# A two-layer hybrid network in one kernel: read products of two batches interleaved, old rows put earlier, last additions shared with GpSimd

## The chip, the cores and the metric

The kernel runs on one core of a Trainium2 chip. The core has five engines with instruction queues of their own: TensorE (PE; its weight loads are listed as PEld), VectorE (DVE), ScalarE (ACT), GpSimd (POOL) and SyncE (SP), which here only issues the stores. The metric is the device time of one launch in microseconds. Lower is better.

## What is computed

The input x has 4 batches of 512 rows of 256 numbers, all float32. Seven blocks follow one another, each of which adds its result to x: latent attention, a ternary feed-forward, cosine attention, the feed-forward again, gated linear attention, a *workspace block*, attention with low-rank adapters (the *adapter stage*), and the workspace block again. Only the workspace block is touched. Cut to what matters:

```
for _ in range(2):                                   # two rounds
    logits = rms(x, w_pre) @ compete_w.T + compete_b
    vals, idx = top_k(swapaxes(logits, 1, 2), 4)     # 4 rows chosen for each of 16 slots
    written = softmax(vals) * (x @ write_w.T + write_b)[idx]    (summed over the 4)
    ws = rms(ws + written, w_post)
    q, k, v = x @ wq.T, ws @ wk.T, ws @ wv.T         # 4 heads, keys and values are the 16 slots
    att = softmax(q k / sqrt(64))
    x = rms(x + (att v) @ out_w.T + out_b, w_post)
```

The block's input is the layer norm of the running x, and its output is added to the running x.

## The kernel before

`last_stages` (in the launch's last third) runs three programs one behind the other on every engine: the first workspace stage ("wsa"), the adapter stage, and the second workspace stage ("wsb"), which alone is given `out` and stores the result. Each engine has one queue, written out by hand; semaphores order the engines.

A workspace stage keeps the running x in `x` and the block's own rows in `xf` (the buffer appears in the profile as cos_wq), as 16 tiles of 128 rows by 256, 4 tiles to a batch. It runs WS_NB = 2 rounds. Round r works as follows on all four batches at once: turn the rows (`turn`, transposes L2289, copied by ScalarE in round 0 and by VectorE at L2045 in round 1), bid (`bid`, L2309), spread the row scales (L2299), select four rows for each slot, write the slots, fold the keys and values into small matrices, scores (L2385), turn the scores (L2393), take the maximum off (`shift`, VectorE), exponents (ScalarE), `divide` (VectorE), turn the probabilities (`turn_probs`, L2399, with the copy L2270 by ScalarE into `attT`), and read.

Reading adds the probabilities times the folded values to the old rows, in PSUM. A batch has two banks, `WS_TURN_BANKS[b]`, of two tiles each. `put_rows` (L2405) multiplies two tiles of old rows by the identity into one bank and so starts the sum. A bank is free at different times: the *early half* of each batch is put before the probabilities are turned, the *late half*, `WS_LATE_HALF[b]`, in `read`, because its bank holds turned scores (banks 2 and 3, for batches 0 and 2) or turned probabilities (banks 4 and 5, for batches 1 and 3) until then. The folded values and the probabilities of two batches, a pair, share the partitions of one buffer: the first batch has rows 0 to 63, the second rows 64 to 127. A float32 product is two instructions on TensorE, so a batch is read by 4 products, 8 instructions (L2413), of 64 rows each, and `put_rows` is 2 instructions.

Behind a batch's read, ScalarE squares and sums its four tiles from PSUM (`mean_squares`, L2228), GpSimd makes the row scales (`row_scales`, L2033 and L2035), and VectorE scales each tile (`norm_sum`, L2128). In round 0 the scaled tile goes to `xf` and the next round begins. In round 1 it stays in PSUM, and VectorE adds the four tiles to `x` with two additions (L2136); with `out` the batch is then stored by SyncE (L2008). The order of VectorE's queue is batch by batch: four scalings, two additions, then what the hooks put behind a batch. In the first stage these hooks are the adapter stage's row statistics (L61 and on) behind batches 0 and 2 and its normalised rows (L2673) behind batch 1.

The adapter stage opens on TensorE with 44 filler products (`keep_busy`, L2867), which first wait for batch 0's addition, then turns the rows (L2878) and makes q and k (L2888, four instructions for each tile, copied by ScalarE). GpSimd and VectorE rotate two tiles of q and k each (L2645, L2649, L2654).

At the very end GpSimd clears each semaphore of these stages (L54), 120 of them.

Of the kernel before, what the change touches and what calls it, by code (L numbers as in the profile page):

```python
# [9 lines left out]
ALU = mybir.AluOpType  # L10
# [4 lines left out]
P = 128  # L15
B, S, D = 4, 512, 256
TI = S // P
# [1877 lines left out]
WS_S, WS_K, WS_NB, WS_H = 16, 4, 2, 4  # L1895
# [12 lines left out]
WS_LATE_HALF = (1, 0, 1, 0)  # L1908
# [25 lines left out]
def workspace_programs(k, g, slots, ps, tag, early, out=None, free=None, hooks={}):  # L1934


    x, ident = g["x"], g["ident"]
    own, shared = slots.own, slots.shared

    def hook(name, *args):  # L1940
        if name in hooks:
            hooks[name](*args)
# [4 lines left out]
    xf = g["cos_wq"][:, :, :].rearrange("p c d -> p (c d)").rearrange("p (n d) -> p n d", d=D)  # L1947
# [25 lines left out]
    nb_w = shared("nb", [P, 2, D])  # L1973
# [6 lines left out]
    attT = shared("attT", [P, 2, S])  # L1980
# [3 lines left out]
             "written", "wsum_ready", "wss_ready", "wsr_ready", "ws_ready", "wt_ready", "wsT_ready", "kv_ready",  # L1984
             "kbd_ready", "vbd_ready", "m_ready", "m_copied", "cb_ready", "cb_copied", "nb_ready", "nb_copied",
             "a_ready", "a_copied", "at_ready", "ash_ready", "ae_ready", "att_ready", "pt_ready", "attT_ready",
             "xb_ready", "m2_ready", "r2_ready", "x_ready", "stored")
    s = {n: k.sem(f"{tag}_{n}") for n in names}
    bias = g["ws_in_b"]

    def tiles(b):
        return slice(b * TI, (b + 1) * TI)

    def bank(n):
        return ps[:, n, :]
# [4 lines left out]
    def read_tile(b, i):  # L2000
        return bank(read_bank(b, i // 2))[:, (i % 2) * D:(i % 2 + 1) * D]

    def by_sync(sp):
        if out is None:
            return
        for b in range(B):
            sp.wait_ge(s["x_ready"], b + 1)
            sp.dma_start(out[b, :, :].rearrange("(i p) d -> p i d", p=P), x[:, tiles(b), :])\  # L2008
              .then_inc(s["stored"], 16)
        sp.wait_ge(s["stored"], 16 * B)  # L2010
# [21 lines left out]
    def row_scales(pool, kind, b):  # L2032
        pool.tensor_tensor(mse[:, kind, tiles(b)], msq[:, kind, tiles(b)], g["ws_eps"][:, 0:TI], ALU.add)  # L2033
        pool.drain()  # L2034
        return pool.tensor_tensor(inv[:, kind, tiles(b)], mse[:, kind, tiles(b)], g["neg_half"][:, 0:TI], ALU.pow)  # L2035

    def first_scales(pool, b):
        pool.wait_ge(s["msq_ready"], b + 1)
        row_scales(pool, 0, b).then_inc(s["inv_ready"], 1)

    def by_vector(dve):
        def copy_turned(r, b):
# [80 lines left out]
        def norm_sum(r, b):  # L2123
            dve.wait_ge(s["r2_ready"], r * B + b + 1)
            for i in range(TI):
                n = b * TI + i
                rows_out = xf[:, n, :] if r + 1 < WS_NB else read_tile(b, i)
                last = dve.scalar_tensor_tensor(rows_out, read_tile(b, i), inv[:, 1, n:n + 1],  # L2128
                                                g["ws_post"][:, :], ALU.mult, ALU.mult)
            if r + 1 < WS_NB:  # L2130
                last.then_inc(s["xf_ready"], 1)
                return
            dve.drain()
            for h in range(2):
                at = b * TI + 2 * h
                last = dve.tensor_tensor(x[:, at:at + 2, :],  # L2136
                                         bank(read_bank(b, h)).rearrange("p (i d) -> p i d", i=2),
                                         x[:, at:at + 2, :], ALU.add)
            last.then_inc(s["x_ready"], 1)
# [41 lines left out]
    def by_gpsimd(pool):  # L2181
        nh, eps = g["neg_half"], g["ws_eps"]

        def slot_scales(r):
            pool.wait_ge(s["wss_ready"], r + 1)
            pool.tensor_tensor(wse[:, :], wss[:, :], eps[:, 0:1], ALU.add)
            pool.drain()
            pool.tensor_tensor(wsr[:, :], wse[:, :], nh[:, 0:1], ALU.pow).then_inc(s["wsr_ready"], 1)

        if early == 0:  # L2190
            pool.memset(vbd[:, :, :, :, :], 0.0)
            invert_variance(pool, 0)
            invert_variance(pool, 1)
            for b in range(B):
                if b + 2 < B:
                    invert_variance(pool, b + 2)
                first_scales(pool, b)
        else:
            for b in range(early, B):
                invert_variance(pool, b)  # L2200
                first_scales(pool, b)
        hook("gpsimd_opened", pool)
        for r in range(WS_NB):
            if r > 0:
                for b in range(B):
                    pool.wait_ge(s["msq_ready"], r * B + b + 1)
                    row_scales(pool, 0, b).then_inc(s["inv_ready"], 1)
            slot_scales(r)
            if r + 1 < WS_NB:
                pool.wait_ge(s["ws_ready"], r + 1)  # L2210
                pool.tensor_tensor(wsb[:, :], ws[:, :], g["ws_write_b"][:, :], ALU.add).then_inc(s["wsb_ready"], 1)
            for b in range(B):
                pool.wait_ge(s["m2_ready"], r * B + b + 1)
                row_scales(pool, 1, b).then_inc(s["r2_ready"], 1)
                if r + 1 == WS_NB:
                    hook("gpsimd_after_batch", pool, b)
            pool.drain()

    def by_scalar(act):
# [55 lines left out]
    def by_tensor(pe):  # L2275
# [120 lines left out]
        def turn_probs(r, q):  # L2396
            pe.wait_ge(s["att_ready"], 2 * r + q + 1)
            for i in range(TI):
                last = pe.transpose(bank(4 + q)[:, i * P:(i + 1) * P], att[:, q, i, :], ident[:, :])  # L2399
            last.then_inc(s["pt_ready"], 1)  # L2400

        def put_rows(r, b, half):

            at = b * TI + 2 * half
            pe.matmul(bank(read_bank(b, half)), ident[:, :], xf[:, at:at + 2, :].rearrange("p i d -> p (i d)"),  # L2405
                      start=True, stop=False)

        def read(r, b):
            q, b2 = b // 2, b % 2
            pe.wait_ge(s["attT_ready"], 2 * r + q + 1)  # L2410
            put_rows(r, b, WS_LATE_HALF[b])
            for i in range(TI):
                last = pe.matmul(read_tile(b, i), attT[64 * b2:64 * b2 + 64, q, i * P:(i + 1) * P],  # L2413
                                 nb_w[64 * b2:64 * b2 + 64, q, :], start=False, stop=(i % 2 == 1))
            last.then_inc(s["xb_ready"], 1)

        if early == 0:
            keep_busy(48, 7)
        for r in range(WS_NB):
            for b in range(B):  # L2420
                turn(r, b)
            bid(r)
            spread_scales(r)
            select(r)
            write(r)
            fold_outputs(r)
            scores(r, 0)
            scores(r, 1)
            turn_scores(r, 0)
            turn_scores(r, 1)  # L2430
            pe.wait_ge(s["nb_copied"], r + 1)
            for b in range(B):
                put_rows(r, b, 1 - WS_LATE_HALF[b])
            turn_probs(r, 0)
            turn_probs(r, 1)
            for b in range(B):
                read(r, b)

    return {"s": s, "by_sync": by_sync, "by_vector": by_vector, "by_gpsimd": by_gpsimd, "by_scalar": by_scalar,
            "by_tensor": by_tensor, "statistics": statistics, "scale_rows": scale_rows,  # L2440
# [835 lines left out]
```

## Time and profile before

| | before |
|---|---|
| median of 3 runs | 2189.97 us (2189.81 to 2190.53) |
| the profiled execution's own time | 2190.11 us |
| its span in the profile | 2188.4 us, 30020 instructions |
| mean granted TensorE clock | 0.969 |
| busy: PE, DVE, ACT, POOL | 1965.3, 1023.3, 812.9, 515.5 us |

The time of an execution is 1.7 us more than its span. "Busy" is the union of an engine's instructions over the span. Times in the rows are microseconds from the span's start, those of single instructions in a group's mean are nanoseconds. A row of the timeline has the start, the duration from the first instruction of a merged run to the end of its last, the engine, the line, the operation, out<-in with shapes, the number of instructions, and in brackets how long the engine was idle before and for whom. The clock column is 1.00 at 2.4 GHz and 0.50 at 1.2 GHz.

### The profile page before, as it was taken

How to read it: one execution, taken by the hardware profiler on the slowest of the kernel's cores; microseconds unless marked ns; L12 is line 12 of the kernel's file. 1: busy time of each engine (PE TensorE's matmuls, PEld its weight loads, DVE VectorE, ACT ScalarE, POOL GpSimd, SP SyncE). 2: the span in 40 equal slices, each digit the busy share in tenths (PEclk: the TensorE clock that was granted, in tenths of full speed). 3: DMA queues.
4: the chain of work that ended last, by engine and by line, in shares of the span. 5: the costliest groups of instructions: out<-in, count | busy, mean ns of one | idle time of the engine just before them, and what ended most of it. 6: DMA issues, size and time to landing. Idle time of an engine off the chain costs nothing. (4 is left out here: it accounts for less than half of the span.)

```text
span 2188.4 us, 30020 instructions
## 1 busy us (share of the span) xinstructions
PE 1965.3 (90%) x11522; PEld 1251.4 (57%) x11522; DVE 1023.3 (47%) x2231; ACT 812.9 (37%) x1786; POOL 515.5 (24%) x617
## 2 busy tenths in 40 slices
PE   6999999999899999999999999669857899999885
PEld 4556666566566766676677667523235554545653
DVE  4555555545223233333243322259955565556444
ACT  2554535545234233323332333135413234445332
POOL 2332322323001011111111010026631143542221
PEclk9999999999999999999999999879979999999998
DMA  5000000000200000000000000020000000000001
GB/s 224 1 1 1 1 1 1 1 1 1 74 1 1 1 1 1 1 1 1 1 1 1 1 1 1 1 69 0 0 1 1 1 1 1 1 1 2 1 1 39
DMA packets 9773, 24.01 MB, mean 11 GB/s; under 512 B 2449, under 2 KB 6305, under 8 KB 8865
## 3 DMA queue, kind: packets, MB, share of 16 engines
q1 hardware_dynamic: 8336, 18.92, 2.4%
q10 hardware_dynamic: 1296, 3.18, 0.4%
q8 instruction: 93, 1.52, 0.3%
q14 instruction: 48, 0.39, 0.1%
HBM read 20.00 MB, written 2.10 MB: 10 GB/s over the span
## 5 line engine op out<-in xcount | busy, mean ns | idle before, releaser
L1429 PEld LDWEIGHTS cos_ps<-cos_vx,cos_probs 128*128 128x128 f32 x2048 | 238.8, 191 | 33.6 <-issue 28.7
L1429 PE MATMUL cos_ps<-cos_vx,cos_probs 128*128 128x129 f32 x2048 | 239.8, 275 | 4.2 <-DVE cos_on L1158 4.2
L1420 PE MATMUL cos_ps<-lead_room,cos_kT 128*128 128x512 f32 x512 | 232.0, 598 | 7.4 <-PEq L50 6.1
L1322 ACT ACTIVATE cos_probs<-cos_ps 128x512 f32<-128x512 f32 x256 | 150.9, 598 | 186.7 <-PE cos_ps L1420 185.9
L671 ACT ACTIVATE probs<-sc,nmax 128x512 f32<-128x512 f32 (+3 forms) x256 | 132.3, 524 | 168.8 <-DVE nmax L525 166.7
L1244 POOL TENSOR_TENSOR cos_qrs<-cos_qse,neg_half 128x4 f32<-128x4 f32 x59 | 59.4, 1006 | 511.9 <-DVE cos_qse L1140 511.9
L780 PE MATMUL sc<-kT,qT 128*128 128x512 f32 (+3 forms) x512 | 172.2, 458 | 3.9 <-DVE probsT L537 2.6
L1420 PEld LDWEIGHTS cos_ps<-lead_room,cos_kT 128*128 128x128 f32 x512 | 94.8, 192 | 104.2 <-issue 101.5
L2743 DVE TENSOR_REDUCE cos_wq<-tail_ps 128x2 f32<-128x1024 f32 (+3 forms) x128 | 101.8, 823 | 82.4 <-PE tail_ps L2983 81.3
L1138 DVE TENSOR_REDUCE cos_qss<-cos_qsq 128x4 f32<-128x512 f32 x59 | 40.5, 686 | 194.4 <-ACT cos_qsq L1301 194.4
L752 PE MATMUL pq<-xnT,wap 128*128 128x512 f32 x256 | 124.9, 611 | 3.5 <-DVE swp L517 3.5
L525 DVE TENSOR_REDUCE nmax<-sc 128x1 f32<-128x512 f32 (+3 forms) x256 | 111.9, 483 | 28.8 <-PE sc L782 26.3
L2971 PE MATMUL tail_ps<-lora_kT,lora_qT 32*128 32x256 f32 (+3 forms) x512 | 105.8, 490 | 13.9 <-DVE cos_wq L2743 4.3
L1451 PE MATMUL cos_ps<-cos_wout,cos_onT 128*128 128x256 f32 x512 | 115.7, 379 | 0.0
L780 PEld LDWEIGHTS sc<-kT,qT 128*128 128x128 f32 x512 | 80.9, 192 | 60.1 <-issue 58.8
L1293 ACT ACTIVATE lead_room<-cos_ps 128x512 f32<-128x512 f32 x59 | 35.2, 597 | 211.9 <-PE cos_ps L1399 211.9
L1408 PE MATMUL cos_ps<-cos_wq,lead_room 128*128 128x512 f32 x236 | 111.0, 592 | 0.0
L2847 ACT ACTIVATE room<-tail_ps 128x768 f32<-128x768 f32 (+1 forms) x96 | 84.6, 881 | 68.8 <-PE tail_ps L2976 68.5
L605 POOL TENSOR_TENSOR rot<-swp,ropeT 128x512 f32<-128x512 f32 x32 | 40.6, 1267 | 272.2 <-DVE swp L517 272.2
L2976 PE MATMUL tail_ps<-lora_qT,lora_kT 32*128 32x256 f32 (+3 forms) x512 | 104.2, 484 | 0.0
L1451 PEld LDWEIGHTS cos_ps<-cos_wout,cos_onT 128*128 128x128 f32 x512 | 95.2, 190 | 13.2 <-issue 1.6
L1697 POOL TENSOR_TENSOR gla_qs<-gla_st,gla_qT 128x512 f32<-128x512 f32 x64 | 82.6, 1313 | 74.3 <-DVE gla_st L1637 74.3
(431 smaller groups left out, 3444.6 us busy)
## 6 DMA issues: line engine op xcount, KB each, us to landing
onT<-in_mla_wqT SPq DMA_DIRECT2D x1, 2048.0 KB, 9.8
lead_room<-in_mla_wo SPq DMA_DIRECT2D x1, 2048.0 KB, 20.1
cos_wq<-in_cos_wq SPq DMA_DIRECT2D x1, 2048.0 KB, 25.7
cos_wout<-in_cos_wout SPq DMA_DIRECT2D x1, 2048.0 KB, 7.4
out<-x SPq DMA_DIRECT2D x4, 512.0 KB, 2.9
x<-in_x SPq DMA_DIRECT2D x1, 1536.0 KB, 15.3
wq_pe<-in_mla_wq_pe ACTq DMA_DIRECT2D x1, 1024.0 KB, 14.8
x<-in_x SPq DMA_DIRECT2D x1, 512.0 KB, 4.2
```

What stands on the lines that cost most here:

```text
L525: red = dve.tensor_reduce(nmax[:, j, qi:qi + 1], sc[:, j, at:at + (qi + 1) * P], AX.X, ALU.max, negate=True)
L671: ex = act.activation(probs[:, j, at:at + (qi + 1) * P], sc[:, j, at:at + (qi + 1) * P], ACT.Exp, bias=nmax[:, j, qi:qi + 1], accum_out=ls ...
L752: last = pe.matmul(pq[:, :], wap[:, c, p, kind, :], xnT[:, b % 2, c, :], start=(c == 0), stop=(c == DC - 1))
L780: pe.matmul(sc[:, j, at:at + (qi + 1) * P], qT[:, n % 2, j, qi * P:(qi + 1) * P], kT[:, b % 2, j, 0:(qi + 1) * P], start=True, stop=False)
L1322: act.activation(probs[:, n % 2, kj, :], ps[:, kj, :], ACT.Exp).then_inc(s["e_done"], 1)
L1408: last = pe.matmul(ps[:, banks["project", b, u], :], xnT[:, b % 2, c, i * P:(i + 1) * P], wq[:, c, 512 * hq:512 * (hq + 1)], start=(c == 0 ...
L1420: pe.matmul(ps[:, kj, :], kT[:, b % 2, kj * P:(kj + 1) * P], qT[:, hq % 2, h % 4, :], start=True, stop=True).then_inc(s["s_ready"], 1)
L1429: last = pe.matmul(po[:, qi // 2, qi % 2, :], probs[:, n % 2, kj, qi * P:(qi + 1) * P], vx[:, b % 2, kj, :], start=(kj == 0), stop=(kj == ...
L1451: last = pe.matmul(y[i], onT[:, n % 2, a, :], wout[:, 8 * half + a, :], start=(half == 0 and a == 0), stop=(half == 1 and a == 7))
L2743: last = dve.tensor_reduce(qs[:, batch % 2, qi, h:h + 2, LORA_HD], ps[:, at:at + 2, col:col + n], AX.X, ALU.max, negate=True)
L2971: pe.matmul(ps[:, at + j, col:col + w], qT[r:r + LORA_SLOT, qi * P:(qi + 1) * P], kT[r:r + LORA_SLOT, n % 2, 0:w], start=True, stop=False)
L2976: turned = pe.matmul(ps[:, at + 2 + j, col:col + w], kT[r:r + LORA_SLOT, t % 2, kj * P:(kj + 1) * P], qT2[r:r + LORA_SLOT, kj * P:], start ...
```

## The change

Three things, in both workspace stages unless said otherwise.

1. `read` is replaced by `read_pair`: for each of the four tiles the product of the pair's first batch and that of its second alternate, instead of all four of one batch and then all four of the next. Each batch still signals `xb_ready` on its last product.
2. The late half of batches 0 and 2 is put before `turn_probs` of its pair, behind a wait for `ash_ready` (the shifted scores have been taken out of that bank). The late half of batches 1 and 3 stays right ahead of the pair's read.
3. In the last round of the second stage alone, the scaled tiles 2 and 3 of a batch are written to `xf` and not to PSUM; VectorE does one addition (tiles 0 and 1) and GpSimd the other (`add_half`, tiles 2 and 3). GpSimd's additions stand one batch late in its queue: behind the row scales of batch b comes the addition of batch b - 1, and that of batch 3 at the end. SyncE waits for both before it stores a batch. Each stage has two more semaphores.

```
-             "xb_ready", "m2_ready", "r2_ready", "x_ready", "stored")
+             "xb_ready", "m2_ready", "r2_ready", "x_ready", "stored", "sums_scaled", "x_added")
...
             sp.wait_ge(s["x_ready"], b + 1)
+            sp.wait_ge(s["x_added"], b + 1)
...
+    def add_half(pool, b):
+        if out is None:
+            return
+        pool.wait_ge(s["sums_scaled"], b + 1)
+        at = slice(b * TI + 2, b * TI + 4)
+        pool.tensor_tensor(x[:, at, :], xf[:, at, :], x[:, at, :], ALU.add).then_inc(s["x_added"], 1)
...
-                rows_out = xf[:, n, :] if r + 1 < WS_NB else read_tile(b, i)
+                to_rows = r + 1 < WS_NB or (out is not None and i >= 2)
+                rows_out = xf[:, n, :] if to_rows else read_tile(b, i)
...
+            if out is not None:
+                last.then_inc(s["sums_scaled"], 1)
             dve.drain()
-            for h in range(2):
+            for h in range(2 if out is None else 1):
...
                     hook("gpsimd_after_batch", pool, b)
+                    if b > 0:
+                        add_half(pool, b - 1)
+            if r + 1 == WS_NB:
+                add_half(pool, B - 1)
...
-        def read(r, b):
-            q, b2 = b // 2, b % 2
+        def read_pair(r, q):
             pe.wait_ge(s["attT_ready"], 2 * r + q + 1)
-            put_rows(r, b, WS_LATE_HALF[b])
+            put_rows(r, 2 * q + 1, WS_LATE_HALF[2 * q + 1])
             for i in range(TI):
-                last = pe.matmul(read_tile(b, i), attT[64 * b2:64 * b2 + 64, q, i * P:(i + 1) * P],
-                                 nb_w[64 * b2:64 * b2 + 64, q, :], start=False, stop=(i % 2 == 1))
-            last.then_inc(s["xb_ready"], 1)
+                for b2 in range(2):
+                    last = pe.matmul(read_tile(2 * q + b2, i), attT[64 * b2:64 * b2 + 64, q, i * P:(i + 1) * P],
+                                     nb_w[64 * b2:64 * b2 + 64, q, :], start=False, stop=(i % 2 == 1))
+                    if i == TI - 1:
+                        last.then_inc(s["xb_ready"], 1)
...
-            turn_probs(r, 0)
-            turn_probs(r, 1)
-            for b in range(B):
-                read(r, b)
+            for q in range(2):
+                pe.wait_ge(s["ash_ready"], 2 * r + q + 1)
+                put_rows(r, 2 * q, WS_LATE_HALF[2 * q])
+                turn_probs(r, q)
+            for q in range(2):
+                read_pair(r, q)
```

## Rows read from the trace of the kernel before

**Rows 1.** Waits, 2100 to 2121 us: who waited for whom, us in total, times, longest.
```profile
ACT room L2228 <- PE tail_ps L2413: 5.9, 4, 2.2
```

**Rows 2.** Timeline, first workspace stage, round 0: puts, reads, first squares.
```profile
1675.55 1.99 PE L2413 MATMUL tail_ps<-room 64*128 64x256 f32 x8
...
1677.47 1.13 PE L2405 MATMUL tail_ps<-cos_wq,ident 128*128 128x512 f32 x2
1677.58 0.38 ACT L2228 ACTIVATE room<-tail_ps 128x256 f32<-128x256 f32 x1 [2.19 <-PE tail_ps L2413]
...
1678.53 1.99 PE L2413 MATMUL tail_ps<-room 64*128 64x256 f32 x8
```

**Rows 3.** Timeline, the same round's end: last batch's squares, copies, bid.
```profile
1686.51 0.38 ACT L2228 ACTIVATE room<-tail_ps 128x256 f32<-128x256 f32 x1 [1.23 <-PE tail_ps L2413]
...
1688.34 0.42 ACT L2228 ACTIVATE room<-cos_wq 128x256 f32<-128x256 f32 x1
...
1691.47 4.88 DVE L2045 COPY cos_wout<-tail_ps 128x512 f32<-128x512 f32 x8
...
1696.49 3.64 PE L2309 MATMUL tail_ps<-cos_wout,wsp_cw 128*32 128x512 f32 x16 [3.97 <-DVE cos_wout L2045]
```

**Rows 4.** Timeline, 1701 to 1703 us: the adapter folds and the fillers behind.
```profile
1701.41 1.14 PE L2696 MATMUL tail_ps<-lora_b,lora_am 64*128 64x256 f32 x8
...
1702.48 0.34 PE L2279 MATMUL tail_ps<-mask_b,ident_b 128*128 128x128 bf16 x3
```

**Rows 5.** Timeline, second stage, round 1: early puts, turned probabilities, late put.
```profile
2151.10 3.60 PE L2405 MATMUL tail_ps<-cos_wq,ident 128*128 128x512 f32 x8
...
2155.10 0.66 PE L2399 MATMUL tail_ps<-ident,room 128*128 128x128 f32 x4 [0.40 <-DVE room L2119]
...
2157.38 1.02 PE L2405 MATMUL tail_ps<-cos_wq,ident 128*128 128x512 f32 x2
```

**Rows 6.** Timeline, second stage, round 1: batch 0's chain, and the last additions.
```profile
2160.36 0.38 ACT L2228 ACTIVATE room<-tail_ps 128x256 f32<-128x256 f32 x1 [2.19 <-PE tail_ps L2413]
...
2162.18 0.20 POOL L2033 TENSOR_TENSOR wsp_mse<-wsp_msq,ws_eps 128x4 f32<-128x4 f32 x1 [23.18 <-ACT room L2228]
...
2163.58 1.67 DVE L2128 SCALAR_TENSOR_TENSOR tail_ps<-tail_ps,wsp_inv,ws_post 128x256 f32<-128x256 f32 x4 [6.75 <-POOL wsp_inv L2035]
...
2165.32 1.29 DVE L2136 TENSOR_TENSOR x<-tail_ps,x 128x512 f32<-128x512 f32 x2
...
2174.69 1.29 DVE L2136 TENSOR_TENSOR x<-tail_ps,x 128x512 f32<-128x512 f32 x2
```

**Rows 7.** Timeline, first stage's last round and the adapter stage's opening.
```profile
1741.76 1.41 DVE L61 BATCH_NORM_STATS2 lora_stats<-x 128x6 f32<-128x256 f32 x4
...
1744.26 2.63 PE L2867 MATMUL tail_ps<-mask_b,ident_b 128*128 128x128 bf16 x44
...
1748.34 1.09 PE L2878 MATMUL tail_ps<-ident,lead_room 128*128 128x128 f32 x8 [1.45 <-DVE lead_room L2673]
...
1750.26 7.11 PE L2888 MATMUL tail_ps<-lead_room,lora_xnT 128*128 128x512 f32 x16 [0.83 <-ACT lora_xnT L2824]
...
1754.49 1.30 POOL L2645 TENSOR_TENSOR lora_rot<-lead_room,lora_rope 128x512 f32<-128x512 f32 x1
...
1755.07 1.29 DVE L2136 TENSOR_TENSOR x<-tail_ps,x 128x512 f32<-128x512 f32 x2
...
1756.49 1.21 DVE L2645 TENSOR_TENSOR room<-lead_room,lora_rope 128x512 f32<-128x512 f32 x1
...
1757.29 1.00 POOL L2654 TENSOR_TENSOR cos_wq<-lora_rot 128x256 f32<-128x256 f32 x1
```

**Rows 8.** Busy time by window: length, PE, PEld, DVE, ACT, POOL, then clock, DMA, GB/s.
```profile
1694.10:1697.60 3.50, 1.11 (x8) 0.46 (x12) 2.24 (x4) 1.86 (x9) 2.41 (x4) 0.51 0.02 5
```

**Rows 9.** Page, part 6, the stores: KB each, us from issue to landing.
```profile
out<-x SPq DMA_DIRECT2D x4, 512.0 KB, 2.9
```

**Rows 10.** Clears of semaphores, 2170 to 2189 us: ns min/median/max, first and last start.
```profile
L54 POOLq EVENT_SEMAPHORE_RANGE_CLEAR  x120: 44/44/44, 2179.3 to 2188.0; - x120
```

## The prediction

> **What bounds the kernel now.** The edits touch the two workspace stages alone, some 1620 to 1756 us and 2050 to 2188 us, of two rounds each. So I read, in this order, who waits for whom at the end of a round, the timeline there, and the granted clock. The waits at the end of the second stage's round 0 show ScalarE waiting for TensorE's read products once for each of the four batches, 5.9 us in all [rows 1]. The timeline says why: per batch TensorE puts the late half of the old rows (L2405, 1678.53 - 1677.47 = 1.06 us) and then reads (L2413, 1677.47 - 1675.55 = 1.92 us); the sum of 2.98 us is also the distance of ScalarE's batches, (1686.51 - 1677.58) / 3 = 2.98 us [rows 2, 3]. Where ScalarE does not wait, its four squares of a batch take 1688.34 - 1686.51 = 1.83 us. So in round 0 of either stage TensorE sets the end, and all that follows hangs on the last batch: VectorE scales batch 3, copies the turned rows for 4.88 us, and TensorE, idle for 3.97 us, bids [rows 3]. In the last round of all VectorE sets the end: scalings and both additions come every (2174.69 - 2165.32) / 3 = 3.12 us, which is more than TensorE's 2.98 [rows 6].
>
> **The read by pairs.** The 8 products of a batch use 64 of the array's 128 rows and stream one behind the other: 1.92 us, which I read as eight times 0.213 us (half of the 0.427 us that a 512-column product takes, below) and 0.21 us before the next kind. After the change 16 products alternate between upper and lower 64 rows. The trace has this shape in this order: the adapter folds (L2696), 64x256, alternating halves, into two banks. Eight of them take 1702.48 - 1701.41 = 1.07 us to the next instruction, four times 0.213 and the same 0.21 [rows 2, 4]. So a pair costs 8 x 0.213 + 0.21 = 1.92 us, as much as one batch does now. The bounds are 1.92 (full overlap) and 16 x 0.213 + 0.21 = 3.62 us (none); I take 1.92, since the folds are the nearest row.
>
> In the first stage's times: batches 0 and 1 are read from 1675.55 to 1677.47, so batch 0 is ready when it is now; 2 and 3 are done at 1677.47 + 1.06 + 1.92 = 1680.45. ScalarE wants batch 2 at 1677.58 + 2 x 1.83 = 1681.24, so it waits no more, and its batch 3 starts at 1683.07 instead of 1686.51, 3.44 us sooner. GpSimd (2163.58 - 2162.18 = 1.40 us a batch) and VectorE (1.67) keep up with 1.83; the copies behind them move whole [rows 2, 3, 6]. The rows are turned for the next round with more room between, which may lower the clock; at half of it a batch takes 1.7 us to turn, and VectorE comes to batch 3 only after six of its eight copies (3.7 us). Two such rounds: **6.88 us**.
>
> **Rows that enter sooner.** The late halves of batches 0 and 2 move ahead of the turned probabilities. The early instructions start at 2151.10 in steps of 3.60 us for eight less the last one's tail, 0.427 each, so the tenth ends at 2151.10 + 10 x 0.427 = 2155.37, and the first transposes, now at 2155.10, come 0.3 us late. ScalarE's copy of them then ends near 2156.7 and is needed only behind the put that stays (2157.38). The new wait, on the shifted scores, never holds: VectorE shifts both pairs before it divides the first, whose transposes these are. Cost 0; without the cover it is 0.3 us a round. A gain has no place, as the read starts behind the second pair's transposes now and then [rows 5].
>
> **The last round of the first stage.** VectorE is the bound here, with additions and the adapter stage's statistics in one queue until 1755.07 + 1.29 = 1756.36. It starts with batch 0, which is not sooner: gain 0, though the last reads end 6 us earlier. A price can come from the clock. The 44 fillers, now at 1744.25 for 2.63 us right behind the reads, start as soon as batch 0's addition is done (1741.7, the statistics follow it) and end at 1744.3; the transposes still come at 1748.34. TensorE then idles for 4.0 us instead of 1.45 [rows 7]. Behind the idle time of 3.97 us ahead of the bid the granted clock stood at 0.51, the 1.2 GHz level [rows 3, 8]. If it falls here too, the transposes end about 0.9 us late, and a product pair of q and k (four instructions, 1.71 us) takes 3.4 us. The first two feed GpSimd's rotation (1754.49) and VectorE's (1756.49); their copies are ready some 0.9 us behind the products, near 1750.26 + 1.71 + 0.9 = 1752.9 and 1754.6, so 1.6 and 1.9 us ahead. Bounds: 0 (covered) and 5 us (all 16 products at half clock); I take **-0.3 us**, near the cover.
>
> **The last round of all.** VectorE's batch becomes 1.67 + 0.07 + 0.69 + 0.09 = 2.52 us, with one addition of 0.69 in place of two. GpSimd adds the other half from SBUF, 128x512: 1.30 us by L2645 of that shape; from above 2 x 1.00 = 2.00 us (L2654, half as wide), from below VectorE's 0.69 [rows 6, 7]. Behind the new wait in GpSimd's queue stand the row scales of the batches after, for which VectorE waits. With ScalarE's batches from 2160.36 every 1.83: GpSimd has scales 0 and 1 by 2163.58 and 2165.41, adds 0 until 2166.7, scales 2 (2168.1), adds 1 (2169.4), scales 3 (2170.8), adds 2 (2172.1). VectorE starts batch 3 at 2163.58 + 3 x 2.52 = 2171.14, its scalings end at 2172.81, and GpSimd's last addition at 2174.15. Now the last one ends at 2174.69 + 1.29 = 2175.98: **1.83 us** sooner. At 2.00 us an addition GpSimd becomes the bound and ends at 2176.3, 0.3 us later than now.
>
> Does GpSimd slow VectorE? Two additions from PSUM took VectorE 1.29 us while GpSimd multiplied from 1754.49 on, as long as in the last round; a product of two SBUF operands beside GpSimd took 1.21 us [rows 6, 7]. The Trainium skill's GPSIMD Engine Reference (Key points) has GpSimd share its SBUF interfaces with VectorE and contend with VectorE instructions that have two SBUF inputs. By that rule the changed loop is clear, since its scalings and additions take their other operand from PSUM; did they count as such, the second half of the batch would grow and the 1.83 us shrink toward nothing. The trace agrees with the rule.
>
> The stores come at least 1.9 us apart instead of 3.1, and one takes 2.9 us to land; if none may overlap, the last is some 0.9 us late. I take 0, since much of 2.9 us for half a megabyte must be the way there [rows 9]. Four more semaphores are cleared at the end, where 120 take 2188.0 - 2179.3 = 8.7 us: 4 x 0.073 = **-0.29 us** [rows 10].
>
> **Sum.** 6.88 + 1.83 - 0.3 - 0.29 = 8.1 us off the profiled execution: its span from 2188.4 to 2180.3, its time from 2190.11 to 2182.0. The median of the runs shown is 0.14 us under that time; I forecast 2181.9.
>
> **Rivals.**
> - *Each change of half drains the array*, with the 0.21 us seen at a change of kind [rows 2, 4]. Eight changes in a pair: 3.41 + 8 x 0.21 = 5.1 us. ScalarE's batch 3 in round 0 then starts at 1675.55 + 2 x 5.1 + 1.06 + 0.11 + 1.83 = 1688.75, 2.2 us later (twice); the first stage's last round starts 3.2 later, the last one ends 1.8 later, clears 0.3: 2190.1 + 9.7 = 2199.8, slower. It decides from a pair of 3.7 us up, where the gains at the round ends are used up by the late first batch. Against it: eight folds in 1.07 us leave no room for a drain. The skill's page TensorEngine Tiling (Key Properties) lets a change of tiling mode drain the engine, but not a change of tile; by it the pair stays at 1.92. Chance 0.04.
> - *No overlap, no drain*: 3.62 us a pair. Round 0 gains 0.7 twice, the first stage's last round loses 1.7, the last gains 1.2, clears 0.3: 2189.5, no change. The same row speaks against it. 0.05.
> - *The clock takes part back*: the adapter stage opens at 1.2 GHz for longer than the cover lasts. For it: 4.0 us of idle time, as ahead of the bid [rows 3, 8]. Against it: 1.6 to 1.9 us of cover. 2 to 5 us: 2184 to 2187. 0.15.
> - *The clock gives*: bid and spread of scales run from 1696.49 to 1701.41 at 1.2 GHz now [rows 3, 4, 8]; other gaps ahead of them might keep 2.4 GHz, worth some 2 us a round: 2178 to 2180. Against it: the idle time right before the bid stays. 0.06.
> - *The last additions give nothing*, by a slower GpSimd or stores in line: 2183 to 2184. 0.10.
> - *As forecast*, 2180.5 to 2183.3: 0.60.
>
> **Numbers.** A difference under 0.2% (4.4 us) counts as none: the line is at 2185.6. Faster are the forecast, the last additions, the clock that gives, and 0.12 of the clock that takes: 0.88. Same: its other 0.03 and no overlap, 0.08. Slower: 0.04. The range of 2179.5 to 2185.5 leaves out the two overlap rivals and the ends of the two of the clock, 0.16 together.
>
> **What would show it.** The 16 reads of a pair in about 2 us and two batches ready together; ScalarE's squares every 1.83 us, with no wait after the first; the copies of the turned rows 3.4 us sooner behind batch 0's read; in the last round VectorE every 2.5 us, GpSimd's additions near 1.3 us and the last of them ending the work; 124 clears. It would be wrong by a first batch that is ready later than now, by VectorE slowed while GpSimd adds, by TensorE, GpSimd or VectorE waiting longer at the adapter stage's opening, or by stretches of 0.50 where the clock now is 1.00.

## The result, and the profile after

The changed kernel took 2186.62 us (median of 12 executions, 2181.72 to 2190.11), the kernel before beside it on the same chip 2191.17 us (12, 2188.73 to 2195.46). The medians differ by 4.55 us (0.21%), the means by 5.3 us. The ratio of the means is 0.9976, 95% interval 0.9966 to 0.9985: faster by 0.24%, and the prediction's line for a change, 0.2%, lies inside that interval. The forecast was 2181.9 us, 2179.5 to 2185.5: the direction is right, the time 4.7 us too low and 1.1 us outside the range. The profiled execution took 2188.3 us, its span is 2186.4 us.

First the steps one by one. Waits of the changed kernel from 2100 to 2121 us, the answer to [rows 1]:

```profile
ACT room L2244 <- PE tail_ps L2430: 2.2, 1, 2.2
```

ScalarE waits for read products once, no longer four times. The timeline of the changed kernel, first workspace stage, round 0, answers to [rows 2, 3]:

```profile
1672.30 4.46 PE L2421 MATMUL tail_ps<-cos_wq,ident 128*128 128x512 f32 x10
...
1679.54 2.00 PE L2430 MATMUL tail_ps<-room 64*128 64x256 f32 x16
...
1681.46 1.12 PE L2421 MATMUL tail_ps<-cos_wq,ident 128*128 128x512 f32 x2
1681.56 0.39 ACT L2244 ACTIVATE room<-tail_ps 128x256 f32<-128x256 f32 x1 [2.18 <-PE tail_ps L2430]
...
1682.52 2.00 PE L2430 MATMUL tail_ps<-room 64*128 64x256 f32 x16
...
1687.06 0.39 ACT L2244 ACTIVATE room<-tail_ps 128x256 f32<-128x256 f32 x1
...
1692.02 4.88 DVE L2054 COPY cos_wout<-tail_ps 128x512 f32<-128x512 f32 x8
...
1697.04 3.59 PE L2325 MATMUL tail_ps<-cos_wout,wsp_cw 128*32 128x512 f32 x16 [3.97 <-DVE cos_wout L2054]
```

Sixteen products of a pair take 1681.46 - 1679.54 = 1.92 us to the next instruction, just the sum's figure, and ScalarE's squares come every (1687.06 - 1681.56) / 3 = 1.83 us, batch by batch. From batch 0's squares to the copies it is 1692.02 - 1681.56 = 10.46 us; before it was 1691.47 - 1677.58 = 13.89 [rows 2, 3]. The round gives 3.43 us of the 3.44. But the copies themselves start 0.55 us *later* than in [rows 3]: this execution came into the stage late. The last round of all answers to [rows 5, 6]:

```profile
2150.54 4.46 PE L2421 MATMUL tail_ps<-cos_wq,ident 128*128 128x512 f32 x10
...
2159.80 0.39 ACT L2244 ACTIVATE room<-tail_ps 128x256 f32<-128x256 f32 x1 [2.18 <-PE tail_ps L2430]
...
2163.03 0.88 DVE L2138 SCALAR_TENSOR_TENSOR tail_ps<-tail_ps,wsp_inv,ws_post 128x256 f32<-128x256 f32 x2 [6.75 <-POOL wsp_inv L2036]
...
2163.82 0.87 DVE L2138 SCALAR_TENSOR_TENSOR cos_wq<-tail_ps,wsp_inv,ws_post 128x256 f32<-128x256 f32 x2
...
2164.78 0.69 DVE L2148 TENSOR_TENSOR x<-tail_ps,x 128x512 f32<-128x512 f32 x1
2164.78 1.26 POOL L2048 TENSOR_TENSOR x<-cos_wq,x 128x512 f32<-128x512 f32 x1
...
2165.56 0.88 DVE L2138 SCALAR_TENSOR_TENSOR tail_ps<-tail_ps,wsp_inv,ws_post 128x256 f32<-128x256 f32 x2
...
2172.36 1.26 POOL L2048 TENSOR_TENSOR x<-cos_wq,x 128x512 f32<-128x512 f32 x1 [1.23 <-DVE cos_wq L2138]
```

VectorE's batch is 2165.56 - 2163.03 = 2.53 us (2.52 in the sum), GpSimd's addition 1.26 (1.30). Two scalings take 0.88 us where that addition runs beside them for 0.48 us (2165.56) and 0.88 without it (2163.03), so no slowing of VectorE shows. The last addition ends 2172.36 + 1.26 - 2159.80 = 13.82 us behind the first squares, before 2174.69 + 1.29 - 2160.36 = 15.62 [rows 6]: 1.80 us sooner, the sum says 1.83. The clears of the changed kernel and, from its page, its stores:

```profile
L54 POOLq EVENT_SEMAPHORE_RANGE_CLEAR  x124: 44/44/44, 2177.0 to 2186.0; - x124
```
```profile
out<-x SPq DMA_DIRECT2D x4, 512.0 KB, 3.0
```

Clearing takes 9.0 us instead of 8.7 [rows 10], and a store 3.0 instead of 2.9 [rows 9]. So each of these terms has its size. The term that has not is the clock's, at the adapter stage's opening, here in the timeline of the changed kernel, beside [rows 7],

```profile
1742.76 2.63 PE L2887 MATMUL tail_ps<-mask_b,ident_b 128*128 128x128 bf16 x44 [3.36 <-DVE x L2148]
...
1749.37 1.97 PE L2898 MATMUL tail_ps<-ident,lead_room 128*128 128x128 f32 x8 [3.98 <-DVE lead_room L2693]
...
1752.12 8.56 PE L2908 MATMUL tail_ps<-lead_room,lora_xnT 128*128 128x512 f32 x16 [0.78 <-ACT lora_xnT L2844]
...
1756.24 1.29 POOL L2665 TENSOR_TENSOR lora_rot<-lead_room,lora_rope 128x512 f32<-128x512 f32 x1 [0.69 <-ACT lead_room L2846]
```

and its windows there (busy time per engine, then the clock):

```profile
1742.80:1745.40 2.60, 2.59 (x44) 2.42 (x44) 2.45 (x11) 0.84 (x4) 0.42 (x1) 1.00 0.00 0
...
1749.30:1751.40 2.10, 1.97 (x8) 1.57 (x8) 2.03 (x6) 0.62 (x2) 2.02 (x2) 0.50 0.00 0
```

The fillers end early, TensorE idles 3.98 us (4.0 foreseen), and the turns run at a granted clock of 0.50, which is 1.2 GHz: 1.97 us instead of 1.09, q and k 8.56 instead of 7.11. GpSimd's rotation now waits 0.69 us for its copy. The larger part is that code which the change does not touch ran later. Windows of the kernel before, and below it of the changed kernel, over the block ahead of the first workspace stage:

```profile
1600.00:1620.00 20.00, 9.84 (x24) 5.21 (x20) 4.18 (x6) 4.97 (x6) 2.48 (x2) 0.69 0.00 0
1400.00:1620.00 220.00, 162.43 (x512) 59.97 (x512) 158.51 (x236) 78.99 (x123) 98.21 (x78) 0.88 0.05 18
```
```profile
1600.00:1620.00 20.00, 9.21 (x16) 4.23 (x17) 6.17 (x11) 4.97 (x6) 4.97 (x4) 0.54 0.00 0
1400.00:1620.00 220.00, 164.16 (x504) 59.61 (x505) 156.96 (x233) 79.13 (x123) 98.20 (x78) 0.85 0.06 18
```

Clock 0.85 instead of 0.88, eight products fewer done by 1620 us, and the first row statistics of the workspace stage start at 1620.46 us before and here at

```profile
1625.58 1.41 DVE L61 BATCH_NORM_STATS2 wsp_stats<-x 128x6 f32<-128x256 f32 x4 [1.99 <-PEq L50]
```

5.12 us late in unchanged code. The stages themselves, from these statistics to the end of the span, take 2186.4 - 1625.6 = 560.8 us against 2188.4 - 1620.5 = 567.9: 7.1 us less. The experiments ask whether the 5 us and the lost 1 us belong to the change.

### The profile page after: what moved, and what is told of

It is laid out like the page before. It is cut to its first block and busy times, and to the rows that moved or that the text cites. A ratio compares the mean times of both kernels' runs of the same rounds, so it can differ in the third digit from the quotient of the medians.

```text
span 2186.4 us, 30028 instructions
## 1 busy us (share of the span) xinstructions
PE 1958.1 (90%) x11522; PEld 1247.1 (57%) x11522; DVE 1021.8 (47%) x2227; ACT 815.1 (37%) x1786; POOL 521.1 (24%) x621
```

## Experiments

Two kinds of kernel were run. Full ones compute everything. *Cut* ones leave out the first five blocks: x and the weights are loaded and the three last stages start at once (first row statistics at some 22 to 23 us), so they show the stages without what lies ahead. "Mean" is over all executions of a run; a profiled execution is one of them. Times of runs are medians, with the lowest and highest in brackets.

**The stages alone, before and after.** The cut kernel before, and the cut changed kernel:

> The kernel before without its first 1620 us: latent, cosine and gated attention and both feed-forwards are left out, x and the weights are loaded, and the two workspace stages and the adapter stage run on the input x itself. It is the yardstick for the other cut kernels: some 575 us (2188.4 - 1620.5 us of stages and 10 to 20 us of loads). Spread theory (the 8.1 us are there, and what the whole kernel's medians miss comes from the stretch ahead of the first workspace stage, 5.1 us longer in the profile after): the executions of this kernel lie within 2 us of each other, where those of the whole kernel spread over 7. Clock theory (part of the gain goes back to the granted clock inside these stages): they spread by more than 3 us.

> The changed kernel with the same first stages left out. Spread theory: 8 us (7.5 to 8.6) less than the cut kernel before. Clock theory: 4.5 to 6 us less, with the missing part in stretches at 1.2 GHz at the opening of the adapter stage (TensorE's wait between the fillers and the transposes 4.0 us instead of 1.5).

593.41 us (589.88 to 595.31, 5 executions) and 583.51 (581.50 to 586.42, 4). The spread theory's 2 us is wrong: the executions of one kernel lie 5.4 and 4.9 us apart inside these stages too. The medians differ by 9.9 us, the means by 9.1, more than either theory says. The profiled spans are 588.2 and 579.8: 8.4 us less, where the sum has 8.1. The granted clock of the two is not the same. From their pages, 40 equal slices each, the kernel before first (a digit is the granted clock in tenths; 8 or less is a slice with a stretch at 1.2 GHz):

```profile
PEclk9979997999987998999999999999999999979995
```
```profile
PEclk9979987998798998999999999999999998889975
```

But every stretch outside the changed rounds takes the same time within 0.2 us, so the 8.4 us are the changed rounds'. Both were run once more, on further chips:

> The cut kernel before once more: five executions had a mean of 592.9 us, and eight of the cut changed kernel 584.4 us. Chance theory: the joint mean of this one stays within 592 to 594 us, 8 to 9 us over the cut changed kernel. Systematic theory (the changed stages lose more to the clock than the stages before): 590 to 591 us, 6 us over it.

> The cut changed kernel once more. Its four executions so far had a mean of 583.7 us, 9.2 us under the five of the cut kernel before. Chance theory: the joint mean stays 7.5 to 9.5 us under it. Systematic theory: it goes to 5 to 7 us.

590.25 (588.07 to 593.25) and 585.08 (583.77 to 586.39). Taken together 9 executions before have a mean of 591.8 and 8 after of 584.4: 7.4 us less, with a 95% interval of some 2.2 us either way. That lies between the two theories and decides nothing. The profiled spans of this second pair, 586.4 and 582.0, are only 4.4 us apart. Most of the missing 4 us are one stretch of unchanged code behind the first stage's last round, which took the kernel before 48.97 us here and 52.89 in its first profile (the changed kernel 53.06 and 52.93).

**The whole kernels again.** The changed kernel twice and the kernel before once more, on three further chips:

> The changed kernel as it is, once more, to set its mean against more executions of the kernel before on the same chip. Chance theory (the stages give 8.4 us, and the 12 executions on record were unlucky in the unchanged stretch ahead): the mean of these lies 7 to 9 us under that of the kernel before. Systematic theory (something outside the stages takes 3 us back): 4 to 6 us under it.

> The changed kernel once more, for six more executions beside the kernel before. Two profiled executions at the same position of the clock's changes differ by 8.0 us, two at different positions by 2.0 us. Chance theory: with these the difference of the means comes to 6.5 to 8 us. Systematic theory (other positions cost the changed kernel more than the kernel before): it stays at 5 to 6.5 us.

> The kernel before, unchanged, for a second profiled execution of it. Three profiled executions of the changed kernel reach the first workspace stage, in code that is the same in both kernels, at 1620.8, 1624.7 and 1625.6 us; the one of the kernel before at 1620.5. Chance theory: this one lies anywhere from 1620 to 1626, and the mean of its executions at 2191.9 within 2 us. Systematic theory (the change makes the stretch ahead longer): 1620.5 again, within 0.5 us.

The changed one took 2184.30 (ratio 0.9961, 0.9947 to 0.9975) and 2184.10 (0.9962, 0.9949 to 0.9975), in the mean 8.4 and 8.1 us under the kernel before on the same chip; the kernel before against itself has 0.9993 (0.9984 to 1.0002). The windows of the changed kernel's first repeat show the clock of the kernel before in the unchanged block, not that of the execution above:

```profile
1600.00:1620.00 20.00, 10.18 (x24) 5.24 (x20) 4.40 (x8) 4.97 (x6) 2.48 (x2) 0.69 0.00 0
1400.00:1620.00 220.00, 162.53 (x512) 60.01 (x512) 158.75 (x237) 78.97 (x123) 98.18 (x78) 0.88 0.06 18
```

Its statistics start at 1620.80 and its span is 2180.3, 8.1 us less than the 2188.4 of before; the stages take 559.5 us instead of 567.9, 8.4 us less as in the first pair of cut kernels. In the other repeats the statistics start at 1624.71 (changed) and 1622.18 (before), and the stages take 559.7 and 567.9 us. The changed kernel alone thus enters the stages anywhere from 1620.8 to 1625.6 us, so its late entry on record is scatter; the two profiles of the kernel before are 1.7 us apart. Over all runs 71 executions of the kernel before have a mean of 2192.1 (standard deviation 2.3), 24 of the changed one 2185.3 (2.8): 6.8 us less, within 1.3. All three expectations come out as the chance theories say.

**The parts alone**, in three cut kernels: the pairs and the sooner rows, with all last additions on VectorE (the third part of the change is taken out); the sooner rows alone; and all but the pairs. First the edit of the rows alone, in the kernel before:

```
-            put_rows(r, b, WS_LATE_HALF[b])
+            if b2 == 1:
+                put_rows(r, b, WS_LATE_HALF[b])
...
+                pe.wait_ge(s["ash_ready"], 2 * r + q + 1)
+                put_rows(r, 2 * q, WS_LATE_HALF[2 * q])
                 turn_probs(r, q)
```

And the single reads, which stand in place of `read_pair`'s products in the changed kernel:

```
+            for b2 in range(2):
+                if b2 == 1:
+                    put_rows(r, 2 * q + 1, WS_LATE_HALF[2 * q + 1])
+                for i in range(TI):
+                    last = pe.matmul(read_tile(2 * q + b2, i), attT[64 * b2:64 * b2 + 64, q, i * P:(i + 1) * P],
+                                     nb_w[64 * b2:64 * b2 + 64, q, :], start=False, stop=(i % 2 == 1))
+                last.then_inc(s["xb_ready"], 1)
```

> Cut kernel with the pairs and the earlier rows, but VectorE does all the last additions as before. My sum: the last round gains nothing (VectorE's 3.12 us a batch from the same start) and no semaphores are added, so 6.9 us less than the cut kernel before and 1.5 us more than the cut changed kernel. Rival: GpSimd's additions were hidden anyway, and it is as quick as the cut changed kernel.

> Cut kernel before with the rows of batches 0 and 2 put sooner and nothing else: batches are read singly. My prediction gave this part no gain of its own. If it has none, this is as slow as the cut kernel before. Rival, seen in the single reads above: batch 0 is ready one put (1.06 us) sooner and batch 3 two puts (2.1 us), so 2.1 us in each round 0 and 1.0 us in each last round where VectorE sets the end: 6.3 us less than the cut kernel before.

> The cut changed kernel without the pairs: rows sooner and the last additions shared, but every batch read singly, batch 0 and 2 ahead of the put that remains. With the rows alone a round 0 took 2.86 us less than before and with the pairs as well 3.46 us. Theory that the pairs pay little: 0.6 us more in each round 0, 0.87 us less in the first stage's last round and 0.4 us less in the last, so within 0.5 us of the cut changed kernel (stages of 559.5 us at the same clock). Rival, my prediction's (all of the 6.9 us come from the pairs): 6 us more than it.

They took 584.31 us (579.62 to 586.83), 585.03 (581.16 to 586.86) and 581.38 (578.91 to 588.88; 580.83 without that slowest one). Single executions of one kernel lie up to 10 us apart, so times can't tell the parts apart. Distances between rows of the timeline can, since they repeat within 0.05 us from profile to profile. All figures are in us, from one profile each, and the last column is a full kernel, further down:

| | before | rows | rows, pairs | rows, additions | changed | best |
|---|---|---|---|---|---|---|
| round 0 (each), early puts to copies | 23.16 | 20.30 | 19.70 | 20.29 | 19.70 | 19.70 |
| first stage's last round, early puts to first squares | 9.27 | 8.41 | 9.27 | 8.41 | 9.27 | 8.41 |
| last round, early puts to last store | 24.91 | 24.06 | 24.91 | 22.81 | 23.16 | 22.75 |
| first row twice, and the others | 80.50 | 73.07 | 73.58 | 71.80 | 71.83 | 70.56 |

The timeline of the rows alone says how they give 2.86 us without any pair (first stage, round 0; the cut kernel's times):

```profile
77.47 1.99 PE L2414 MATMUL tail_ps<-room 64*128 64x256 f32 x8
...
79.39 1.12 PE L2405 MATMUL tail_ps<-cos_wq,ident 128*128 128x512 f32 x2
...
80.45 2.96 PE L2414 MATMUL tail_ps<-room 64*128 64x256 f32 x16
...
83.34 1.12 PE L2405 MATMUL tail_ps<-cos_wq,ident 128*128 128x512 f32 x2
...
84.40 1.99 PE L2414 MATMUL tail_ps<-room 64*128 64x256 f32 x8
```

Batch 0's read has no put ahead of it, and those of batches 1 and 2 follow one another. Their 16 products take 83.34 - 80.45 = 2.89 us to the next instruction, and not 2 x 1.92: two batches on different halves overlap in part even one behind the other. The pairs save another 0.60 us in each round 0. But a pair needs batch 1's put first, so batch 0 is ready 0.86 us later, which the rounds that VectorE bounds pay: 9.27 against 8.41, 23.16 against 22.81. 1.20 gained, 1.21 lost: the pairs as made are worth nothing, the sooner rows nearly all (7.43 us), and the rival of 6 us for the pairs falls. The shared additions give 24.91 - 23.16 = 1.75 us, less 0.3 for the clears. With single reads they give 1.25, as VectorE then waits for GpSimd's row scales. The timeline of the kernel without pairs shows it in the last round:

```profile
559.31 0.88 DVE L2138 SCALAR_TENSOR_TENSOR tail_ps<-tail_ps,wsp_inv,ws_post 128x256 f32<-128x256 f32 x2 [0.52 <-POOL wsp_inv L2036]
```

**The adapter stage's opening.** Is the half clock there a price? 110 fillers in the place of 44, cut:

```
-LORA_FILLERS = {("rows", 0, 0): 44, ("turn", 0, "q"): 24, ("rows", 1, 0): 24,
+LORA_FILLERS = {("rows", 0, 0): 110, ("turn", 0, "q"): 24, ("rows", 1, 0): 24,
```

> The cut changed kernel with 110 fillers instead of 44 at the adapter stage's opening, so that TensorE is busy from batch 0's addition to the first transposes (110 x 0.06 = 6.6 us). Clock theory: 1 to 2 us less than the cut changed kernel, and the clock at 1.00 through the q and k products. Spread theory: the same within 0.5 us.

The fillers do what they should. Timeline of the cut changed kernel, then of the one with 110:

```profile
144.65 1.52 PE L2898 MATMUL tail_ps<-ident,lead_room 128*128 128x128 f32 x8 [2.34 <-DVE lead_room L2693]
146.95 9.60 PE L2908 MATMUL tail_ps<-lead_room,lora_xnT 128*128 128x512 f32 x16 [0.78 <-ACT lora_xnT L2844]
```
```profile
147.55 1.09 PE L2898 MATMUL tail_ps<-ident,lead_room 128*128 128x128 f32 x8 [0.29 <-DVE lead_room L2693]
149.48 7.11 PE L2908 MATMUL tail_ps<-lead_room,lora_xnT 128*128 128x512 f32 x16 [0.83 <-ACT lora_xnT L2844]
```

Turns and q, k take what they take at full clock, yet the time is 583.51 (582.77 to 584.28), to the hundredth the median of the first run of the cut changed kernel, and 0.9 us under the mean of both its runs, within 1.6. From the first squares of the first stage's last round to the first paired score products (the adapter stage's L2976 in the kernel before, whose instructions alternate with L2971's) it takes 50.89 us instead of 52.93, and the next 128 of them take 69.56 instead of 68.16; what is left is within the scatter.

Then the single reads back in the first stage's last round alone, where batch 0 counts, cut and full:

```
-                read_pair(r, q)
+                if out is None and r + 1 == WS_NB:
+                    read_singly(r, q)
+                else:
+                    read_pair(r, q)
```

> The cut changed kernel, but in the first stage's last round batches are read singly, and batch 0 of each pair is read ahead of the put that remains (its own rows are already in), where VectorE sets the end. Both theories: batch 0 is ready one put (1.06 us) sooner and VectorE's whole chain with it, 1.0 us less. Clock theory: 1 us more than that, since TensorE's idle time ahead of the fillers is 2.9 us shorter, so 1.5 to 2.5 us less in all.

> The whole changed kernel with batches read singly in the first stage's last round, batch 0 of each pair ahead of the remaining put. By the cut kernels it should be 2 to 4 us under the changed kernel: 0.9 us from the earlier first batch, the rest from less time at 1.2 GHz at the adapter stage's opening. If that rest was the luck of one execution: 1 us under it.

The cut kernel took 579.30 us (577.43 to 582.14), 4.2 less than the cut changed kernel. The full one took 2184.86 (2179.00 to 2186.93; 0.9956, 0.9941 to 0.9971), beside 2184.30 of the changed kernel on the same chip; in the mean it is 1.0 us under it, far less than the executions scatter, so the full runs do not show the 2 to 4 us. The mechanism is the 0.86 us of the table; the rest sits behind. From those squares to the first paired score products the changed kernel takes 52.99 us and this one 50.08. Windows and folds of the changed kernel (first repeat), and below of this one:

```profile
1773.00:1780.00 7.00, 7.00 (x38) 4.74 (x36) 2.49 (x5) 1.19 (x2) 0.00 (x0) 0.51 0.01 2
...
1778.63 1.71 PE L2716 MATMUL tail_ps<-lora_b,lora_am 64*128 64x256 f32 x8
```
```profile
1773.00:1780.00 7.00, 6.21 (x43) 3.75 (x40) 3.87 (x6) 1.08 (x2) 0.00 (x0) 1.00 0.00 0
...
1775.68 1.13 PE L2729 MATMUL tail_ps<-lora_b,lora_am 64*128 64x256 f32 x8
```

At 1772 us both are at the same products, 0.55 us apart (1772.38 and 1771.83). Then one has 7 us of half clock and the other none: 2.9 us. No line of either kernel was written to decide it, and what decides it is not shown. It is not luck of one execution alone: from those squares to the paired products the six profiles with pairs in that round and 44 fillers take 52.9 to 53.9 us, and four with single reads there 49.8 to 50.1. But three other kernels with single reads take 54.1 to 54.2, and one program, the kernel before, has 52.9 in three profiles (with a clock of 0.72 in this window in the first) and 48.97 in the fourth.

**The bid.** The single reads kept, and 34 fillers placed ahead of the bid in the second rounds, cut and full:

```
+            if r > 0:
+                pe.wait_ge(s["xfT_ready"], r * B + 1)
+                keep_busy(34, WS_TURN_BANKS[0][1])
```

> The cut kernel with single reads in the first stage's last round, and 34 fillers on TensorE in the idle time ahead of the bid of each second round, behind batch 0's copies (2.0 us at 2.4 GHz, 3.6 at 1.2). Clock theory: the bid and the spread of the scales then run at 1.00 in most executions, 4.9 us shorter by 2 us in each stage, so 2 to 4 us under the kernel with single reads alone (579.5 us mean), and the executions lie closer together. If the fillers come too late to change the clock: the same within 1 us, or 0.7 us a round later where they run at 1.2 GHz and delay the bid.

> The same two additions in the whole kernel: 2 to 4 us under the whole kernel with single reads (mean 2183.7 us), if the cut kernel shows it; otherwise within 1 us of it.

In the full kernel's timeline the 16 bids take 1.92 us where they took 3.59 above:

```profile
1691.14 2.07 PE L2295 MATMUL tail_ps<-mask_b,ident_b 128*128 128x128 bf16 x34 [0.29 <-DVE cos_wout L2054]
1694.82 1.92 PE L2328 MATMUL tail_ps<-cos_wout,wsp_cw 128*32 128x512 f32 x16 [1.60 <-DVE cos_wout L2054]
```

From the bid to the copy of the new slots it is 17.41 us instead of 19.64 and 19.10, some 3.9 us in the two rounds, of which 2.7 are left at the early puts of these rounds. But the full kernel took 2183.35 (2181.96 to 2184.12, 0.9956) against 2184.86 without, the cut one 578.53 against 579.30: within the scatter. In the full kernel's profile the squares to the first paired products took 54.19 us (50.08) and the next 128 products 69.62 (68.21). Two such gains and neither reached the end: this shows where they went in these executions, not that they always go.

**The best of the parts.** Pairs in both rounds 0, where TensorE sets the end, and single reads in both last rounds, where batch 0 does (the edit above without `out is None and`):

> The whole changed kernel with pairs in both rounds 0 and single reads in both last rounds. Of the first the cut kernel showed 0.87 us; the second should give 0.4 us, since VectorE starts its chain 0.87 us sooner but waits 0.46 us for batch 1. So 1.3 us under the changed kernel at the same clock, and a mean near 2184.

2179.01 us (2177.69 to 2183.05), 0.9942 (0.9929 to 0.9955), faster than both the kernel before and the changed one: its mean is 5.8 us below the changed kernel's, within some 2.2. By the table 1.3 us of these are mechanism; its profile also goes over the stretch with the dip in 50.10 us. Five executions on one chip don't say how much of that will stay.

## Why the prediction was off

**The mechanism held in its total.** A round 0 gave 3.43 us (3.44 in the sum), the last round 1.75 to 1.80 (1.83), the clears cost 0.3 (0.29). That a pair costs "8 x 0.213 + 0.21 = 1.92 us, as much as one batch does now" is right to the hundredth, and the adapter folds of unlike data were the right row for it. Between profiles whose unchanged stretches take the same time the whole is 8.1 us (full) and 8.4 us (cut), against 8.1. The rivals "drain" and "no overlap" fell with the 1.92 us. "The last additions give nothing" fell: VectorE's batch is 2.53 us while GpSimd adds, with VectorE's additions of 0.69 us beside GpSimd's. By the Trainium skill's GPSIMD Engine Reference (Key points), as the prediction used it, these additions with one operand in PSUM are clear of contention; the trace agrees, and no run here tests two operands in SBUF beside GpSimd's additions. The stores, 2.5 us apart and 3.0 us each, came through without a visible delay. One sum among the rivals is off: without overlap the last round would gain 1.83 - 1.70 = 0.1 us and not 1.2, which makes 2190.6 instead of 2189.5 and leaves that rival at no change.

**The step that failed is the last: the sum was set off against one execution, and the range had no term for the clock's scatter.** "Its time from 2190.11 to 2182.0" took three executions within 0.7 us for the kernel's time. 71 executions have a mean of 2192.1 and reach from 2188.7 to 2199.0, so the anchor was 2 us low. With the right one, 2192.1 - 8.1 = 2184.0, still 1.3 us under the changed kernel's mean of 2185.3 and 2.6 under the median on record. Of the 1.3, 0.2 lie outside the span: the profiled times of the whole changed kernel are 1.9 to 2.0 us over their spans, those of the whole kernel before 1.7 to 1.8, and the sum left this at 1.7. A range about it needed the 2 to 3 us by which executions of one kernel differ. The profile of the kernel before gave the warning: a clock of 0.88 over 220 us in a block nobody touches can mean that some microseconds depend on where the dips fall. The Trainium skill's TensorE: Matmul & The Clock Gate (Part 1) calls the time until full clock at a kernel's start variable from run to run and its cost under 1% of a typical kernel. What scatters here lies in the kernel's course and not at its start, by 2.3 us or 0.1%; no run here shows the start by itself.

**The rows that enter sooner** ("Cost 0", "A gain has no place") were priced wrong. The step gave the whole round to the pairs. The gain had a place: the three puts between four reads, of which two go away. The sum was right because both parts stood in one calculation (only batch 3's put lay between the pairs); the division was wrong: 2.86 of 3.46 us a round are the rows'. It also hid that the pairs undo 0.86 us of it in the first stage's last round and 0.35 in the last, which wait for batch 0 ("so batch 0 is ready when it is now" was read as no loss). That is what the best version takes back.

**The clock at the adapter's opening, -0.3 us, was sized too small.** The idle time and the half clock came as told: the turns take 1.5 to 2.0 us in all six profiles with pairs and 44 fillers there, against 1.09 in all four of the kernel before. The cover did not hold. By the prediction's own figures the first copy would come 0.9 + 1.7 = 2.6 us late against 1.6 us of cover, so GpSimd would wait 1.0 us, and it took 0.3. In the profile on record GpSimd's first rotation waits 0.69 us; from its squares to the paired products it takes 53.85 us against 52.93 before, and to the 128th after it 69.06 against 68.22. That would be 1.8 us, between "forecast" and "the clock takes part back". The repeats have 52.99 and 69.06, and 53.14 and 68.16; the cut kernels 52.89 before and 52.93 changed, both 68.16. So the price came to 1.8 us in the profile on record and to nothing that shows in most others, where the kernel before lost as much to a dip further on; its one profile without that dip took 48.97 us. The time on record lies inside the rival's 2184 to 2187, but 5.1 us of that execution's lateness came from unchanged code. 66 more fillers bought nothing measurable.

**What stays open.** Means differ by 6.8 us within 1.3; profiles with equal unchanged stretches differ by 8.1 and 8.4, the second cut pair by 4.4. One thing is not chance: the changed kernel is granted a lower clock. Its mean granted clock is 0.966 over 24 executions against 0.969 over the 59 of the kernel before that list it, in the cut kernels 0.934 (8) against 0.942 (9). That is an estimated 12 and 9 us more at 1.2 GHz, worked out from these means and the times. Much of it costs nothing, as the equal stretches show. Whether it costs the 1.3 us between 6.8 and 8.1, or chance does, these runs can't say.

## What to carry to other kernels

Price a change's parts each alone before crediting the sum to one of them: here the sooner rows were most of the gain, and the pairs nothing until it was limited to the rounds whose *last* batch is waited for. Where a round waits for the first batch instead, anything that makes it wait for its neighbour's data costs. When a change is worth less than 1%, take the kernel's time from many executions, compare profiles whose unchanged stretches take the same time, and give the range the scatter of the clock.

## What the runs showed of the hardware

- One program's executions, all alike in instructions, scatter by 2.3 to 2.8 us (standard deviation, at some 2190 us), and unchanged code reached the same point at 1620.5 to 1625.6 us.
- Of two kernels 0.55 us apart at the same products one met 7 us at 1.2 GHz and the other none, a difference of 2.9 us. One program, the kernel before, took 52.9 us over this stretch in three profiles and 48.97 in a fourth.
- The faster kernel had the lower mean granted clock: 0.966 against 0.969 whole, 0.934 against 0.942 cut.
- Float32 products on 64 rows overlap even at a single change of half: two batches of eight, one behind the other, took 2.89 us, in alternation 1.92, and with a put between them 1.92 each.
- Fillers raised the clock where they stood (q and k 9.60 to 7.11 us, the bids 3.59 to 1.92) with no gain of the whole that these runs can tell from none.
